# Chebyshev attention beside a mixture of experts: GpSimd's low parts behind a VectorE product, and prefix sums by column halves

## The reference, cut to what matters

```
Tq, Tk  = cheb(clip(q / sqrt(8))), cheb(clip(k / sqrt(8)))     # orders 1 to 5 have weights that are not zero
kv_prefix = cumsum over tokens of Tk * v
ks_prefix = cumsum over tokens of Tk.sum(axis=-1)               # one number a head
num = (Tq * beta * kv_prefix).sum over the orders
den = (Tq.sum(axis=-1) * beta * ks_prefix).sum over the orders
out = (num / (den + 1e-7)) @ W_out.T
```

## Time and profile before

| what | value |
|---|---|
| median of 3 runs | 802.78 us (802.03 to 805.84) |
| the profiled execution's own time | 805.15 us |
| its span, first to last instruction | 803.3 us |
| TensorE busy | 575.8 us (72%) |
| VectorE busy | 649.7 us (81%) |
| ScalarE busy | 419.9 us (52%) |
| GpSimd busy | 433.4 us (54%) |

### The profile page before, as it was taken

One profiled execution on the slowest core, in us unless ns is written; L12 is line 12 of the kernel. 1 busy time (PEld: TensorE's weight loads), 2 busy tenths in 40 slices (PEclk: granted clock), 3 DMA queues, 4 the chain that ended last, 5 costly groups with the idle time before them and its releaser, 6 DMA issues.

```text
span 803.3 us, 22093 instructions
## 1 busy us (share of the span) xinstructions
PE 575.8 (72%) x6987; PEld 387.0 (48%) x7049; DVE 649.7 (81%) x1675; ACT 419.9 (52%) x1019; POOL 433.4 (54%) x697
## 2 busy tenths in 40 slices
PE   1889888888887888886134799899999986452231
PEld 0466666666665655664012456555666553231120
DVE  4678888888788778875279899999999999966687
ACT  1465555555454455452023888888988883211011
POOL 3235555555455778773774445444544453778810
PEclk9999999999799999996557999999999997655555
DMA  9999999900000000000122133333333321212201
GB/s 213 364 284 288 288 285 287 257 0 0 1 0 7 16 21 17 20 17 4 40 102 69 32 115 115 123 107 112 113 107 105 107 67 47 53 52 55 69 27 40
DMA packets 126475, 80.84 MB, mean 101 GB/s; under 512 B 10936, under 2 KB 117312, under 8 KB 126400
## 3 DMA queue, kind: packets, MB, share of 16 engines
q1 hardware_dynamic: 121264, 70.89, 29.4%
q0 software_dynamic: 5136, 9.02, 4.1%
HBM read 18.85 MB, written 49.55 MB: 85 GB/s over the span
## 4 chain that ended last, share of the span: by engine, by line
DVE 42%; PE 20%; issue 16%; POOL 13%; ACT 5%; DVEq 1%; DMA 1%; SPq 1%; POOLq 0%; ACTq 0%
POOL experts_sb L561 8%; DVE kv L1356 4%; DVE yts L1383 4%; DVE mneg L1128 3%; DVE kv L1366 3%; PE q_ps L940 3%; DVE yn L1387 3%; DVE kv L1357 2%; POOL xbuf L490 2%; PE y_ps L873 2%; DVE pr L1381 2%; DVE rot L1170 2%; ACT pexp L608 2%; PE m_ps L823 1%; PE m_ps L809 1%
## 5 line engine op out<-in xcount | busy, mean ns | idle before, releaser
L608 ACT ACTIVATE pexp<-e_ps 128x512 f32<-128x512 f32 x128 | 76.4, 597 | 70.8 <-PE e_ps L856 67.6
L1128 DVE TENSOR_REDUCE mneg<-m_ps 128x4 bf16<-128x512 f32 x128 | 84.9, 684 | 18.7 <-PE m_ps L823 18.4
L561 POOL DMA_INDIRECT experts_sb<-ybuf,slots x64 | 64.1, 1002 | 31.2 <-issue 18.8
L1033 PE MATMUL m_ps<-xs,wb 128*128 128x512 f16 x276 | 74.4, 379 | 3.0 <-ACT xs L726 3.0
L490 POOL DMA_INDIRECT xbuf<-x,slots x64 | 64.4, 1006 | 16.6 <-issue 15.4
L996 PE MATMUL y_ps<-kv,tri_sb 128*128 128x432 f32 x64 | 36.3, 653 | 38.3 <-DVE pr L1382 25.2
L873 PE MATMUL y_ps<-pexp,vd 128*32 128x128 f32 x512 | 57.8, 295 | 2.4 <-ACT pexp L608 0.6
L1087 PE MATMUL e_ps<-b_sb,cwt 8*128 8x128 f32 x64 | 16.6, 436 | 52.3 <-ACT cwt L766 52.3
L837 PE MATMUL e_ps<-early 128*128 128x256 bf16 x256 | 51.6, 283 | 0.8 <-DVE early L1213 0.6
L498 POOL COPY xn_all<-early 128x128 f32<-128x128 f32 (+1 forms) x32 | 12.8, 399 | 71.4 <-DVE early L1138 71.4
L555 POOL TENSOR_TENSOR pexp<-rot,pexp 128x512 f16<-128x512 f32 x24 | 28.9, 1204 | 40.3 <-ACT pexp L718 40.1
(11 more groups left out here) (220 smaller groups left out, 2056.0 us busy)
## 6 DMA issues: line engine op xcount, KB each, us to landing
xbuf<-zero_sb SPq DMA_DIRECT2D x71, 256.0 KB, 4.0
ybuf<-zero_sb SPq DMA_DIRECT2D x71, 256.0 KB, 3.6
wb<-experts_sb SPq DMA_DIRECT2D x46, 256.0 KB, 2.3
xs<-xbuf SPq DMA_DIRECT2D x23, 256.0 KB, 2.7
ybuf<-vd SPq DMA_DIRECT2D x23, 256.0 KB, 2.2
experts_sb<-in_experts_w SPq DMA_DIRECT2D x8, 512.0 KB, 6.8
x_all<-in_x SPq DMA_DIRECT2D x8, 256.0 KB, 5.6
xbuf<-x,slots POOLq DMA_INDIRECT x64, 2.3
```

Source lines behind the costliest of these rows:

```text
L561: nc.gpsimd.indirect_dma_start(yg[:, 2 * (B * n + b) + k, :], None, ybuf, bass.IndirectOffsetOnAxis(ap=slots[:, k, B * n + b:B * n + b + 1 ...
L608: nc.scalar.activation(pexp[:, j, :, :], e_ps[j % 2][:, :, :], ACT.Exp, scale=float(D) ** -0.5).then_inc(exp_ready.sem, 1)
L1033: last = nc.tensor.matmul(u_ps[f % 2], wb1[:, i % 2, f, a, :], xg16[:, i % 2, b, :], start=k == 0, stop=k == len(PARTS) - 1)
L1128: nc.vector.tensor_reduce(mneg[:, n.batch, j // 2, (j % 2) * NG:(j % 2) * NG + NG], m_ps[j % 2][:, :, :], AX.X, ALU.max, negate=True).then ...
```

## The change

Two things are changed. GpSimd, ahead of the four low parts of pass i, waits for the key product (line 1356) of tile i+4. And the prefix sums are laid out by column halves: the 144 columns of an order (128 values, 16 head sums) are cut in two halves of 72, each half of all five orders is one TensorE product of 360 columns into a bank of its own, and the two banks adjoin, so that VectorE's carry and VectorE's product each become one instruction over 720 elements. The product is written with the five orders innermost (a step of five elements from one column to the next), and the sum over the orders reads them side by side.

```diff
+HALF = SW // 2
-CHEB1, CHEB2 = 6, 6
+CHEB1, CHEB2 = 6, 5
...
+def halves(ap):
+
+    return ap.rearrange("p j (a w) -> p a j w", a=2)
...
-        pr = sb("pr", [P, ORD, SW])
+        pr = sb("pr", [P, SW, ORD])
...
-        q_ps = bank("q_ps", [P, 2 * NG, P], F16)
         t_ps = bank("t_ps", [P, 4, P])
-        y_ps = bank("y_ps", [P, 4, P])
+        yq_ps = bank("yq_ps", [P, 2, 4 * P])
+        y_ps = yq_ps[:, 0, :].rearrange("p (a b) -> p a b", b=P)
+        q_ps = yq_ps[:, 1, :].bitcast(F16).rearrange("p (a b) -> p a b", b=P)
...
-        cc_ps = [y_ps[:, :, :].rearrange("p a b -> p (a b)"), q_ps[:, :, :].rearrange("p a b -> p (a b)").bitcast(F32)]
+        cc_ps = yq_ps[:, :, 0:ORD * HALF].rearrange("p a (j w) -> p a j w", w=HALF)
...
             def low_parts(i):
 
+                pool.wait_ge(s_keys, keys_steps(i + LEAD) + 4)
                 for f in range(FB):
...
             def sums(c):
 
                 pe.wait_ge(s_keys, keys_steps(c + 1))
-                after(pe, s_outs, CHEB2 * (c - 1) + 2 if c else 0)
-                after(pe, s_carried, 2 * carries(c))
-                nc.tensor.matmul(cc_ps[0][:, 0:3 * SW], tri_sb[:, :], kv[:, c % 2, 0:3 * SW], start=True, stop=True)
-                nc.tensor.matmul(cc_ps[1][:, 0:2 * SW], tri_sb[:, :], kv[:, c % 2, 3 * SW:5 * SW], start=True, stop=True).then_inc(s_summed, 1)
+                after(pe, s_outs, CHEB2 * (c - 1) + 1 if c else 0)
+                after(pe, s_carried, carries(c))
+                keys = kv[:, c % 2, :].rearrange("p (j w) -> p j w", w=SW)
+                for a in range(2):
+                    last = nc.tensor.matmul(cc_ps[:, a, :, :], tri_sb[:, :], keys[:, :, HALF * a:HALF * a + HALF], start=True, stop=True)
+                last.then_inc(s_summed, 1)
...
-                for k, (lo, hi) in enumerate(((0, 3 * SW), (3 * SW, 5 * SW))):
-                    nc.vector.tensor_tensor(kv[0:1, c % 2, lo:hi], kv[0:1, c % 2, lo:hi], cc_ps[k][LAST:LAST + 1, 0:hi - lo], ALU.add).then_inc(s_carried, 1)
+                row = halves(kv[0:1, c % 2, :].rearrange("p (j w) -> p j w", w=SW))
+                nc.vector.tensor_tensor(row, row, cc_ps[LAST:LAST + 1, :, :, :], ALU.add).then_inc(s_carried, 1)
...
-                done(nc.vector.tensor_tensor(pr[:, 0:3, :], q[:, 0:3, :], cc_ps[0][:, 0:3 * SW].rearrange("p (j w) -> p j w", w=SW), ALU.mult), False)
-                done(nc.vector.tensor_tensor(pr[:, 3:5, :], q[:, 3:5, :], cc_ps[1][:, 0:2 * SW].rearrange("p (j w) -> p j w", w=SW), ALU.mult))
-                done(nc.vector.tensor_reduce(nd[:, :], pr[:, :, :].rearrange("p j w -> p w j"), AX.X, ALU.add))
+                done(nc.vector.tensor_tensor(pr[:, :, :].rearrange("p (a w) j -> p a j w", a=2), halves(q), cc_ps[:, :, :, :], ALU.mult))
+                done(nc.vector.tensor_reduce(nd[:, :], pr[:, :, :], AX.X, ALU.add))
```

More of the change, by code:

```diff
@@ L274, in program @@
         d_ps = [e_ps[i][:, :, :].rearrange("p a (h b) -> p (a h) b", b=P) for i in range(2)]
-        cc_ps = [y_ps[:, :, :].rearrange("p a b -> p (a b)"), q_ps[:, :, :].rearrange("p a b -> p (a b)").bitcast(F32)]
+        cc_ps = yq_ps[:, :, 0:ORD * HALF].rearrange("p a (j w) -> p a j w", w=HALF)
         o_ps = p_ps[:, 3 * C:4 * C]
         xt_ps = t_ps[:, :, :].rearrange("p a b -> p (a b)").bitcast(F16)
-        count_ps = y_ps[:, 2:4, :].rearrange("p a b -> p (a b)")
+        count_ps = yq_ps[:, 0, 2 * P:4 * P]
         xbuf = nc.dram_tensor("xbuf", (BLOCKS * SLOT, 2 * C), F16, kind="Internal").ap()
```

## The result

The changed kernel takes 812.38 us in the median (808.1 to 813.43, 6 runs), the kernel before 805.93 in the runs beside it (802.03 to 806.94, 6 runs). The ratio is 1.0068, with a 95% interval of 1.0044 to 1.0093: the change makes the kernel slower, by some 5.5 us by the ratio (3.5 to 7.5); the two medians lie 6.45 apart. 796.7 was forecast, against the 802.78 that the kernel before had in its first 3 runs.

The account below looks back on a forecast made before the run. VectorE was taken as the bound, with a loop through three engines next. Steps 4.7 us less, start 0.8, end 0.6: 6.1 off 802.78 gives 796.7; own range 793.5 to 799.5, 8-in-10 range 791.5 to 803.

Parts of the forecast that it names:

- part 3: Orders innermost: VectorE's sum over orders falls from 1.40 to 0.89 us; the product's strided write costs nothing, staying at 0.92.
- The rival of the dear write: The product's strided write costs 1.40 us inside the loop, making steps 9.82 and the time 807; chance 0.10.
- the dearest bound: Upper bound for the product's strided write on VectorE: the strided read's own price, 1.40 us for 720 elements.
- the row: Line 1153, a VectorE write with a step of 128 bytes: 344 ns for 128 elements, against 347 without stride.
- the slow rival: Same as the rival of the dear write: product at 1.40 us, time 807, chance 0.10.
- The loop: Chain through TensorE, ScalarE and VectorE, including copy, clip, carry and product, setting steps with a carry: 9.45 us, 9.34 after.
- Part 1: GpSimd waits for the key product: it falls from 1.707 to 0.824 us, the division's from 1.15 to 0.29; wait free.
- Part 2: VectorE's carry and product each become one instruction: carry 0.95 us with hand-over (0.06 less), product 0.92 (0.05 less).
- VectorE is the bound: Steady step before the change: VectorE busy 9.39 of 9.66 us, the bound by less than a microsecond.
- the 9.08: Step time in us where no carry is made (three steps), said to be set by ScalarE's own queue.
- the start: Three VectorE iterations ahead of the first pass: gain of 0.3 to 1.9 us, taken as 0.8.
- the end: Two steps from the last block 1 to the store: gain of 0.1 to 1.2 us, taken as 0.6.

Follow-up runs that it names:

- e6_probe: The changed kernel with 18 kinds of VectorE instructions added three times after its last result, to price strides; one execution, only its trace read, no time given.
- e3_wait_only: The kernel before with only GpSimd's wait added: 801.03 us against 804.43, ratio 0.9956.
- e1_runs: The changed kernel with the product written order by order in runs of 72 columns, the sum over orders reading with a step: 799.58 us against 804.43, ratio 0.9932.
- e4_runs_order: e1_runs with VectorE's carry and product moved ahead of the clip: 794.47 us against 804.43 for the kernel before, ratio 0.9875.
- e2_no_wait: The changed kernel without GpSimd's wait: 810.32 us, ratio 1.009 to the kernel before.
- e7_order_only: The kernel before with only the carry and products moved ahead of the clip: 796.2 us against 804.95, ratio 0.989.
- e9_early_copy: e4_runs_order with the attention output's transpose moved ahead of block 1 and its copy ahead of block 1's gelus: 786.37 us against 804.95 for the kernel before, ratio 0.9772.
- e5_after_order: The changed kernel, strided write kept, with carry and product moved ahead of the clip: 796.27 us against 806.52 for the kernel before, ratio 0.989.
- e8_wait_order: The kernel before with GpSimd's wait and the carry and products moved ahead of the clip: 796.33 us against 804.95, ratio 0.9895.

## Why the prediction was wrong

**The step that failed is the choice in part 3**, "Nearest is a VectorE instruction that writes with a step of 128 bytes [...] So I take nothing." The product's write was to cost nothing and cost 0.55 us (1.472 for 0.92). The rival of the dear write, given a chance of 0.10, had the mechanism: at 1.40 the loop was to be 9.82 and the 22 steps 4.4 us longer; the step measured 9.87 and the steps 4.71 longer. Even the dearest bound, 1.40, was a little low; with 1.472 in place of 0.92 the sum of 9.34 becomes 9.89. The comparison behind it set a one-source instruction against one of another kind. By e6_probe the row's like is the same instruction without the step, 285 against 336; with two sources 292 against 375. The row is also short: over its 128 elements a step costs 0.05 and 0.08 us, while over 720 the step of 20 bytes costs 0.90 and 0.54.

**The rule of the Trainium skill (Advanced Engine Details and Errata, SBUF Cachelines)**, that an access to a different line of 16 bytes each time pays, was argued away with that row. e6_probe agrees with it for writes in SBUF: 0.904 at 4 and 8 bytes, 1.102 at 12, 1.422 at 16 and about the same from there on. By the rule the forecast would have been the slow rival's 807; the measured ratio of 1.0068 on 802.78 gives 808.2.

**The loop was right.** It was added up to 9.45, to 9.34 with carry and product joined, and to 9.08 where no carry is made; e3_wait_only measured 9.43, e1_runs 9.30, and the changed kernel's steps without a carry 9.10 (487.55 to 496.65, from clip to clip). With carry and product out of the loop, e4_runs_order has 9.10 in its other steps too. Part 1's collisions went as forecast (0.825 in all tiles, and 0.291 in the median for the division's product), and its wait cost nothing: without it the changed kernel is no faster (e2_no_wait). Part 2's carry of 0.92 measured 0.904. Part 3's sum over orders of 0.89 measured 0.903. With the write undone, e1_runs shows the forecast of 0.8% less as 0.7% less.

**Three things the prediction said too simply.** "VectorE is the bound" of before held only for the phase in which GpSimd met both products: in e7_order_only the queue shrinks by the second collision without any wait. And a low part does not hold up only products with two SBUF inputs: in e2_no_wait it held up a one-source instruction of 0.29 us for 0.84. And the 9.08 was called ScalarE's own queue: in e4_runs_order ScalarE is busy 8.44 of 9.10, and e9_early_copy, with the same work on it in another order, has steps of 8.77. So the 9.08 was a second loop, through ScalarE and TensorE; as a number it was right.

The ends of this pair came near the forecast, the start 0.65 for the 0.8 taken, the end 0.50 for 0.6. That may be chance: e1_runs, with the same wait and the same joined instructions, starts its passes 2.8 us later (445.98) than the changed kernel's profile, and no run shows what either end is worth. What stays open is why the changed kernel's unprofiled runs stand some 2.5 us further off than the profiled pair (5.5 against 3.0). Their mean clock is 0.861 to 0.865 where the profiled run has 0.872; none of them has a profile. Of the profiled executions, those with a mean clock of 0.860 to 0.862 (e1_runs, e4_runs_order, e5_after_order, e7_order_only, e8_wait_order) have a granted clock of 0.50 from 436 to 440 us, about the start of the passes, and those with 0.868 to 0.872 (before, changed, e2_no_wait) have 1.00. So a slower start of the passes may be part of it; that is not shown.

## What to carry to other kernels

A layout that spares one instruction a strided read may hand the stride to another one's write, and both cost about the same here (0.50 us for the read, 0.57 for the write); so ask which of the two stands in the loop that sets the step, and put the stride on the other, as e1_runs does. When an engine idles ahead of a wait, look for instructions behind the wait that don't need it: here moving the carry and the product ahead of the clip was worth more (1.1%) than the whole change was meant to be. And price an operation by an instruction of the same kind and length; a row that differs in sources and scalars can hide exactly the cost that is looked for.

## What the runs showed of the hardware that was not expected

Reading PSUM with a step of 288 bytes cost VectorE nothing (0.904 for 720 elements, line 1487), while writing SBUF with the same step cost 0.53 (1.432, line 1486). A one-source instruction over SBUF loses more by a step of 20 bytes in its write than one with two: 0.534 to 1.436 us against 0.907 to 1.449 for 720 elements.

The first passes' speed differs between executions by the granted clock. The first row is of the kernel before, the second of e1_runs, both from 436 to 440 us (columns as in the earlier trace rows):

```profile
436.00:440.00 4.00, 1.82 (x12) 1.13 (x12) 3.80 (x7) 1.73 (x5) 0.00 (x0) 1.00 0.36 106
```

```profile
436.00:440.00 4.00, 2.47 (x10) 1.44 (x10) 2.77 (x5) 1.57 (x5) 0.00 (x0) 0.50 0.19 57
```

The clock is 1.00, the 2.4 GHz level, in the one and 0.50, the 1.2 GHz level, in the other; and block 0 of the first pass, which starts at 441.48 in both, took 0.82 and 1.46 us. TensorE had been at 0.50 in both from 432 to 436, busy 2.95 and 3.45 of 4 us.

So a microsecond or two at the start of the passes comes and goes between profiles, and the 22 steps, which all run at a clock of 1.00 from 450 us on, are the better measure of a change than the span.
